# Rewriting the border between two layers: two buffers for the recurrence's heads, another order, and products moved from VectorE to GpSimd

## The reference, cut to what matters

```python
x = _layernorm(x + _L0_attn_ref(x, ...))     # causal attention, 16 heads of 8
x = _layernorm(x + _L0_ffn_ref(x, ...))      # soft mixture of 8 experts with 64 slots each
x = _layernorm(x + _L1_attn_ref(x, ...))     # delta rule: a recurrence over the 512 tokens, then an MLP
x = _layernorm(x + _L1_ffn_ref(x, ...))      # gated MLP with ternary weights
```

```python
logits = jnp.einsum('bsd,etd->bset', xn, se)
dispatch = jax.nn.softmax(logits, axis=1)
slots = jnp.einsum('bsd,bset->betd', xn, dispatch)
h = jax.nn.gelu(slots @ w1, approximate=False)
processed = h @ w2
combine = jax.nn.softmax(logits.reshape(b, s, e * t), axis=-1)
out = jnp.einsum('bnd,bsn->bsd', processed.reshape(b, e * t, d), combine)
```

```python
Sk = jnp.einsum('bhkv,bhk->bhv', Sm, ki)
upd = ki[..., :, None] * (vi - Sk)[..., None, :]
Sm = Sm + bi[..., None, None] * upd
oi = jnp.einsum('bhkv,bhk->bhv', Sm, qi)
```

## Time and profile before

| | us |
|---|---|
| median of 3 runs | 1311.79 |
| lowest, highest | 1306.53, 1312.87 |
| the profiled execution | 1302.49 |
| its span, first to last instruction | 1300.8 |

### The profile page before, as it was taken

One profiled execution on the slowest core, in us unless ns is written; L12 is line 12 of the kernel. 1 busy time (PEld: TensorE's weight loads), 2 busy tenths in 40 slices (PEclk: granted clock), 3 DMA queues, 4 the chain that ended last, 5 costly groups with the idle time before them and its releaser, 6 DMA issues.

```text
span 1300.8 us, 19019 instructions
## 1 busy us (share of the span) xinstructions
PE 1117.7 (86%) x6008; PEld 591.0 (45%) x6008; DVE 930.4 (72%) x2129; ACT 620.1 (48%) x1226; POOL 478.3 (37%) x602
## 2 busy tenths in 40 slices
PE   5989989999999999999884821297999999999996
PEld 2434444564445644455351511143545555555453
DVE  4647647477687878878575667998798898898131
ACT  1161736637456374563652300333565565555642
POOL 3040312304154341443303343444647537556310
PEclk8989999999999999999897975698999999999999
DMA  4230210322213323133022257022021120210000
GB/s 116 74 114 10 66 50 10 115 68 83 66 34 114 102 78 99 38 113 81 15 57 73 59 134 198 29 52 59 9 60 45 24 68 16 51 28 9 22 9 8
DMA packets 85043, 79.83 MB, mean 61 GB/s; under 512 B 42096, under 2 KB 62704, under 8 KB 82928
## 3 DMA queue, kind: packets, MB, share of 16 engines
q1 hardware_dynamic: 84976, 79.01, 22.0%
HBM read 43.17 MB, written 35.00 MB: 60 GB/s over the span
## 4 chain that ended last, share of the span: by engine, by line
PE 63%; DVE 17%; issue 7%; ACT 6%; POOL 4%; DMA 3%; ACTq 0%; DVEq 0%; SPq 0%; POOLq 0%
PE ps L1358 15%; PE ps L1339 7%; PE ps L1040 5%; PE ps L1001 5%; PE ps L966 5%; PE ps L1004 3%; PE ps L1011 3%; PE ps L1027 3%; PE ps L1349 3%; DVE arena L1886 2%; ACT arena L1480 2%; PE ps L1089 2%; PE ps L1069 2%; PE ps L1117 2%; PE ps L1099 2%
## 5 line engine op out<-in xcount | busy, mean ns | idle before, releaser
L1886 DVE TENSOR_REDUCE arena<-ps 128x4 f32<-128x512 f32 (+2 forms) x192 | 198.1, 1043 | 49.6 <-PE ps L1004 48.2
L1358 PE MATMUL ps<-arena,late 128*128 128x512 f32 x512 | 227.3, 596 | 0.3 <-ACT arena L1621 0.3
L1453 ACT ACTIVATE arena<-ps 128x512 f32<-128x512 f32 (+2 forms) x200 | 110.1, 568 | 239.3 <-PE ps L966 104.6
L1480 ACT ACTIVATE arena<-ps 128x1024 f32<-128x1024 f32 (+3 forms) x256 | 169.1, 712 | 32.2 <-PE ps L1027 30.9
L784 POOL TENSOR_SCALAR_AFFINE_SELECT arena<-arena 128x512 f32<-128x512 f32 x128 | 87.1, 683 | 237.4 <-ACT arena L1480 236.8
L1358 PEld LDWEIGHTS ps<-arena,late 128*128 128x128 f32 x512 | 96.2, 191 | 114.6 <-issue 112.2
L1621 ACT ACTIVATE arena<-ps,f_s 128x512 f32<-128x512 f32 x128 | 83.2, 687 | 109.3 <-PE ps L1358 98.6
L883 POOL TENSOR_TENSOR arena<-arena 128x256 f32<-128x256 f32 x128 | 93.2, 728 | 66.1 <-ACT e_w L1680 43.3
L1339 PE MATMUL ps<-arena,late 128*128 128x512 f32 x256 | 115.4, 603 | 2.1 <-ACT arena L1621 2.1
L1011 PE MATMUL ps<-mask_qk,ident_b 128*128 128x512 bf16 x340 | 91.7, 396 | 25.3 <-DVE arena L2179 25.3
L966 PE MATMUL ps<-ident,arena 128*128 128x128 f32 (+1 forms) x624 | 95.6, 286 | 18.7 <-ACT arena L1453 12.0
(11 more groups left out here) (186 smaller groups left out, 1882.9 us busy)
## 6 DMA issues: line engine op xcount, KB each, us to landing
qr<-q_rep SPq DMA_DIRECT2D x16, 512.0 KB, 4.0
kr<-k_rep SPq DMA_DIRECT2D x16, 512.0 KB, 4.9
scan_d<-late SPq DMA_DIRECT2D x7, 1104.0 KB
arena<-scan_d SPq DMA_DIRECT2D x12, 552.0 KB, 7.2
q_rep<-hilo SPq DMA_DIRECT2D x24, 256.0 KB, 3.0
k_rep<-hilo SPq DMA_DIRECT2D x24, 256.0 KB, 3.2
proj_d<-arena SPq DMA_DIRECT2D x8, 768.0 KB, 5.1
late<-proj_d SPq DMA_DIRECT2D x8, 768.0 KB, 4.5
```

Of the source, the lines that this page charges most:

```text
L1358: last = pe.matmul(ps[:, ring2.bank(f"{n}{c}"), :], w[:, k, c * P:(c + 1) * P], src[:, k, :], start=(k == 0), stop=(k == HC - 1))
L1453: return act.activation(dst, src(ps[:, bank, :]), func, **kw)
L1480: act.activation(prob[:, gg % 2, 2 * pr:2 * pr + 2, p_off[jt]:p_off[jt] + w], ps[:, bank:bank + 2, 0:w], ACT.Exp).then_inc(p_taken, 1)
L1886: v.tensor_reduce(heads[:, 2 * pr:2 * pr + 2, gs[0]:gs[-1] + 1], ps[:, at:at + 2, 0:len(gs) * w].rearrange("p q (n w) -> p q n w", w=w), X ...
```

## The change

It has four parts.

- **Two heads' buffers.** `heads_last` now serves batches 5 and 7, `heads` the others. Those two have their own `p_mix_late` in the memory of `qr` and their own `p_beta_late`, and their own semaphores (`last_loaded`, `last_stored`). Batch 7's scaling waits for batch 5's store. `raw_h2`, which shares memory with `heads_last`, is loaded after batch 7's store.
- **The slot logits first.** For batch 7 TensorE makes M0 to M3 before L0 to L3, in an order written out with its own table of banks (`border`), interleaved with the expert output and the combination of batch 6. VectorE adds batch 7's `mo` directly from PSUM (`add_last`). The hidden layer of batch 7 lies in the memory of `hilo`.
- **Older heads in the last slot.** In slot 7 VectorE folds batch 3 between the tops and sums its scores at once, makes batch 4's norms before `attend(0)` and folds batch 4 beside the last `attend`s. GpSimd squares batch 4 after its second causal selection and scales it among the last ones. The ternary weights' first three loads are issued before batch 6's store. The store of x2 has its own semaphore and comes after the heads' load.
- **First products on GpSimd.** In every batch the folding's three products `pairs` are made by GpSimd in `scale_heads`, behind the first half of `wu`; `DVE_WY` goes from 12 to 9.

```diff
+        cm = Carve(0, qr.rearrange("p g s -> p (g s)").bitcast(F32))
+        p_mix_late = cm.take(3 * HD, TS)
+        h_T_late = hilo.rearrange("p j h s -> p (j h) s").bitcast(F32)
...
+        border = {(TL, use): bank for use, bank in (
+            ("M0", 0), ("M1", 1), ("M2", 2), ("M3", 3), ("dT0", 6), ("dT1", 7), ("dT2", 0), ("dT3", 1), ("L0", 2), ("sn", 5),
+            ("L1", 3), ("L2", 6), ("slots", 7), ("L3", 0), ("h0", 1), ("h1", 2), ("h2", 3), ("h3", 5), ("cT0", 4), ("cT1", 6),
+            ("cT2", 7), ("cT3", 0), ("pr", 6), ("mo", 7))}
...
+        def beside_last(b):
+            return isinstance(b, int) and b in (B - 3, B - 1)
...
-            return heads_last if isinstance(b, int) and b == B - 2 else heads
+            return heads_last if beside_last(b) else heads
...
-            return b - 1 if isinstance(b, int) and b == B - 1 else b
+            return b - 1 if isinstance(b, int) and b >= B - 2 else b
...
             def load_heads(b):
-                sp.wait_ge(proj_stored, CREDIT + (b + 1) * 48)
-                sp.wait_ge(l_kb, CREDIT + b * 5)
-                sp.dma_start(p_mix.rearrange("p (j d) k -> p j (d k)", j=3),
+                mix, beta = mix_of(b)
+                loaded = last_loaded if beside_last(b) else pre_loaded
+                sp.wait_ge(proj_stored, CREDIT + (b + 1) * 32)
+                if mix is p_mix or b == B - 1:
+                    sp.wait_ge(l_kb, CREDIT + held(b) * 5)
+                else:
+                    sp.wait_ge(p_ready, CREDIT + B * len(p_units))
+                sp.dma_start(mix.rearrange("p (j d) k -> p j (d k)", j=3),
...
             store_heads(B - 5)
             store(B - 3)
+            store_x2(B - 3)
             load_heads(B - 3)
             store_heads(B - 4)
+            load(raw_f1, A["L1_ffn_w1_w"].rearrange("(c p) d -> p c d", p=P), raw_loaded)
+            load(raw_f2, A["L1_ffn_w2_w"].rearrange("(c p) d -> p c d", p=P), raw_loaded)
+            load(raw_w3, A["L1_ffn_w3_w"], raw_loaded)
             store(B - 2)
             load_heads(B - 2)
-            store_heads(B - 3)
+            store_x2(B - 2)
             store(B - 1)
             load_heads(B - 1)
+            store_x2(B - 1)
+            store_heads(B - 3)
...
-            sp.wait_ge(pre_stored, CREDIT + (B - 1) * 16)
+            sp.wait_ge(last_stored, 32)
             for t in range(2):
                 sp.wait_ge(sc_loaded[t], CREDIT + 48)
             load(raw_h2, A["L1_ffn_h2_w"].rearrange("(c p) d -> p c d", p=P), last_raw_loaded)
...
             def scale_heads(b):
...
                 if p is heads:
                     g.wait_ge(pre_stored, CREDIT + held(b) * 16)
+                elif b == B - 1:
+                    g.wait_ge(last_stored, 16)
+                yield g.tensor_tensor(p.kc, by_time(mix, 1), along(r_k), ALU.mult).then_inc(l_kb, 1)
+                yield g.tensor_tensor(p.wu[:, :, 0:HD], by_time(mix, 1), along(p.rb), ALU.mult).then_inc(l_kb, 1)
+                g.wait_ge(l_kb, CREDIT + b * 5 + 2)
+                g.wait_ge(wy_done, CREDIT + (held(b) if p is heads or b == B - 1 else 0) * DVE_WY)
+                for r in range(1, CH):
+                    at = r * (r - 1) // 2
+                    last = g.tensor_tensor(p.pairs[:, :, at:at + r, :], kc[:, :, 0:r, :],
+                                           wc[:, :, r, 0:HD].unsqueeze(2).broadcast_to([P, NC, r, HD]), ALU.mult)
+                yield last.then_inc(pairs_made, 1)
...
+            def last_slot():
...
+                        if (gg, jt) == (0, 1):
+                            squares_heads(B - 4, None)
+                        if (gg, jt) == (3, 0):
+                            scaled = scale_heads(B - 4)
...
+            def border_heads():
+                squares_heads(B - 3, None)
+                for _ in scale_heads(B - 3):
+                    pass
+                score_products(B - 3)
+                squares_heads(B - 2, None)
+                for _ in scale_heads(B - 2):
+                    pass
+                squares_heads(B - 1, None)
+                score_products(B - 2)
+                for _ in scale_heads(B - 1):
+                    pass
+                score_products(B - 1)
...
             def fold_heads(b, o):
-                v.wait_ge(l_kb, CREDIT + (b + 1) * 5)
-                for r in range(1, CH):
-                    at = r * (r - 1) // 2
-                    o.mark(v.tensor_tensor(p.pairs[:, :, at:at + r, :], kc[:, :, 0:r, :],
-                                           wc[:, :, r, 0:HD].unsqueeze(2).broadcast_to([P, NC, r, HD]), ALU.mult))
+                v.wait_ge(pairs_made, CREDIT + b + 1)
                 yield o.mark(v.tensor_reduce(p.gram, p.pairs, X, ALU.add))
+                v.wait_ge(l_kb, CREDIT + b * 5 + 3)
...
+            def border_tokens(fold):
+                b, last = B - 2, B - 1
+                advance(*fold, DVE_WY + 1)
+                sum_scores(B - 4)
+                for t in range(4):
+                    top(last, "M", t)
...
+                add_combined(b)
+                o = start_finish(b)
...
+                make_rms(b, o)
+                norms_heads(B - 3)
+                make_x2(b, o)
+                apply_x1(last)
...
+                fold = fold_of(B - 3)
+                advance(*fold, 4)
+                add_last()
+                o = start_finish(last)
+                make_rms(last, o)
+                norms_heads(B - 2)
+                advance(*fold, DVE_WY + 1)
+                sum_scores(B - 3)
+                make_x2(last, o)
+                fold = fold_of(B - 2)
+                advance(*fold, 6)
+                norms_heads(last)
+                advance(*fold, DVE_WY + 1)
+                sum_scores(b)
+                advance(*fold_of(last), DVE_WY + 1)
+                sum_scores(last)
```

423 lines of the change are left out of this document (328 added, 95 removed).

## The result

The changed kernel takes 1275.4 us (median of four runs, 1274.0 to 1279.7), the kernel before 1312.2: a ratio of 0.973, 95% interval 0.970 to 0.977. Forecast were 1275 and 1264 to 1290. The profiled execution of the changed kernel is one of 1274.0 us, with a span of 1272.3 and a granted clock of 0.944 (before: 1302.5, 1300.8, 0.945).

The account below looks back on a forecast made before the run. The border was taken as bound by one heads buffer passed through four batches and by VectorE's program order. 2.4 + 3 + 32.5 - 1.5 = 36.4 us less gave 1266.1 profiled, scaled to 1275 us; range 1264 to 1290.

Parts of the forecast that it names:

- Slots 4 to 6: Start of these slots: three VectorE products move to GpSimd, ending TensorE's 0.86 us waits; 2.4 us less, ends 0 and 2.6.
- The rival of engines that hold each other up: VectorE and GpSimd multiplying delay each other throughout, so moved products free little: 31.6 us gained, 1280 us; chance 14%.
- Slot 7: Last slot: TensorE's 2.15 us wait goes and shorter gaps may keep 2.4 GHz; 0 to 4 us less, 3 taken.
- The border: From slot 7's residual to the first scan step: two buffers and TensorE's continuous order save 32.5 us.
- Step 1: Border, residual to `mo`: TensorE's work sums to 39.6 us, plus 2.1 for three uncovered ScalarE evacuations; `mo` at 718.9.
- the prediction's signs of being wrong: Last heads' load over 66 us after the residual, repeated ScalarE table loads in steps 1 or 3, scan's first wait over 7.
- Step 2: Border, last tokens after `mo`: `add_last` reads PSUM directly in 1.3 us, finish without x2 takes 4.66; ends at 724.9.
- Step 3: Border, x2 transposes to the last Tanh: 5.77 us, ending at 730.7.
- Step 5: Border, squares and norms to 750.3; the last batch's scaling waits for batch 5's store, taken to land at 750.5.
- Steps 7 and 8: Border, GpSimd's scalings, score products and VectorE's last sum to 764.7, plus 2 us of mutual delay (ends 0 and 3.4): 766.7.
- Step 9: Border's end, copy to the scan tile and first scan step: 4.2 us plus 0.8 for transfers in flight; 771.7.
- `raw_h2`: Scan's eighth chunk: the history load now waits for the last batch's store; 1.5 us lost, bounds 0 and 6.5.

Follow-up runs that it names:

- before, again: The kernel before, unaltered, run once more: 1307.3 us in one execution, where its first profile took 1302.5.

## Why the prediction was right, step by step

**Slots 4 to 6: right.** Forecast 2.4 us less; undisturbed intervals of 81.03, 81.02 and 80.64 stand against 81.82, 81.86 and 81.46, 2.5 in all. The rival of engines that hold each other up would have given 0 here. Its mechanism is real wherever both multiply at the same time (below), but its price isn't: the products on GpSimd freed VectorE all the same.

**Slot 7: the size was wrong**, 1.0 in place of 3, and even this isn't clear of chance: the same stretch takes 63.6 and 61.6 us in the two profiles of before, 62.6 and 62.2 in those of the changed kernel. VectorE's 2.15 us wait went, as forecast. The first two logit records behind it came 2.2 us earlier, counted from the slot's first top, but at the slot's end 1.0 was left. Before, then the changed kernel:

```profile
618.67 0.45 PE L1027 MATMUL ps<-qr,kr 32*128 32x384 f32 x2 [1.20 <-ACT arena L1480]
```

```profile
622.75 0.44 PE L1127 MATMUL ps<-qr,kr 32*128 32x384 f32 x2 [1.20 <-ACT arena L1704]
...
625.57 2.07 PE L1169 MATMUL ps<-slot_T,arena 128*128 128x512 f32 x2
```

The waits for ScalarE just ahead are the same in both (1.20 and 0.47 us), and the clock of the stretch is 0.62 in place of 0.57, with 2.07 us for two logit records as before. One gap less didn't keep the clock; the 0 to 4.8 us for it should have been taken at the low end. A second miss stands beside it: the prediction gave slot 7 about 1 us for the products on GpSimd, and the run that put them back lost 5.5 there. The store of batch 3 was issued at 641.67, near the 640 of the forecast, and cost nothing.

**The border: right in the sum, 94.6 us against 94.5, with errors that cancel.**

| step | forecast | measured |
|---|---|---|
| 1 TensorE's order to `mo` | 41.7 | 38.7 |
| 2 `add_last`, finish | 6.0 | 7.6 |
| 3 x2 to the last Tanh | 5.8 | 7.2 |
| 4 to the squares | 11.3 | 10.2 |
| 5 to the last batch's scaling | 8.5 | 9.6 |
| 6 two scalings, products | 4.9 | 5.0 |
| 7, 8 to the last score sum | 11.3 | 11.9 |
| 9 copy, first scan step | 5.0 | 4.4 |

Step 1 added durations of groups, and these overlap by 0.1 to 0.2 us at each change:

```profile
680.43 0.60 PE L1459 MATMUL ps<-ident,arena 128*128 128x128 f32 x4
680.87 1.06 PE L1207 MATMUL ps<-e_w,arena 128*128 128x128 f32 x8
681.76 1.94 PE L1425 MATMUL ps<-arena,slot_T 128*128 128x512 f32 x4
```

The first two last 0.60 and 1.06, 1.66 together, and from the first's start to the third's it is 1.33. Over the 20 groups of step 1 the overlaps make about 2.5 us; another 1.2 is work counted too long, the transposes above all (eight take 1.04 where twice 0.65 was counted; the 14 groups named there are ten in the terms of its sum). The waits for ScalarE were 2.6 us (0.88, 0.95, 0.78) where 2.1 were taken. One of the prediction's signs of being wrong did show, two table loads of ScalarE within step 1 (at 700.64 and 708.00, 1.28 us each), and the step was short all the same; the other two signs didn't.

Step 2 left out that batch 6's squares land beside it: as the 128x4 instruction of the earlier trace rows did, another of 128x4 stood for 1.82 us, now in the last tokens' chain. It starts 0.18 us into the squares and ends with them (721.93 + 1.82, 721.75 + 1.98). The Trainium skill, page "SBUF — State Buffer", section "Who interferes with whom", says that a VectorE `tensor_scalar` in a two-port mode and a GpSimd instruction hold each other off for the whole of the one that came first; this trace and the run without that overlap (0.17 us) agree with it, though they don't show the instruction's mode. Step 3 left out that TensorE waits 2.51 us for that chain and then has a lower clock; the projections take 5.19 us where they take 3.80 with 35 idle matmuls ahead.

Step 5 was right in rule and time: the scaling waits for batch 5's store, which was issued 61.3 us after the residual (forecast 61.3) and landed 11.9 later. What held the issue is not in the prediction: SP had issued the last heads' loads by 739.98 and then waited for the store of x2, which waits for VectorE (741.18). It is longer in the table only because the squares came a microsecond early.

Steps 7 and 8 were near in time and wrong in the path. The forecast let GpSimd's queue end last (7.8 us of scalings and score products, then the sum of 1.5) and took 2 us for mutual delay, so 11.3. GpSimd's queue took 8.1 and ended at 766.65, 2.3 us before the sum began. What ended last were VectorE's own fold steps:

```profile
759.98 1.40 DVE L2265 TENSOR_TENSOR arena<-arena 128x256 f32<-128x256 f32 x1 [0.35 <-POOL arena L875]
761.41 1.45 DVE L2266 TENSOR_TENSOR arena<-arena 128x256 f32<-128x256 f32 x1
...
762.65 4.00 POOL L888 TENSOR_TENSOR arena<-arena 128x128 f32<-128x128 f32 x4
```

They took 10.3 us in place of 6.3: 3.7 of delay in the two-input steps and 0.35 of waiting. Against the forecast's 9.3 without any delay that is 2.6 more, where 2 were taken. The run with most of the last score products left out gives back 1.8 of this; the rest stands beside the three scalings. Step 9 has 0.2 us over the 4.2 of before, and 0.6 in the repeat, both with `raw_h1` 16 us ahead of the copy, and 1.7 to 2.0 with it 14 to 15 ahead, where 0.8 was taken.

So the rules of the border came out (its waits, their order up to the scaling), and the match to 0.1 us is luck: terms of 3.0 and 0.6 us too much and of 1.6, 1.4 and 0.6 too little lie beneath it.

**`raw_h2`: nothing in this profile, up to 1.2 us in others.** TensorE waited 2.08 us for it, but the history was kept at 789.8, before the eighth chunk's last step ended. In the repeat of the same kernel VectorE does wait there:

```profile
789.18 0.49 DVE L2511 TENSOR_REDUCE arena<-arena 128x64 f32<-128x320 f32 x1 [0.73 <-ACT e_w L1933]
```

and in the nine other versions of the changed kernel that step comes 0.2 to 1.2 us late. So the wait is there, as forecast, at the edge, and 1.5 us were more than any run showed. The 0.8 us of the table came later, between 74 and 194 us after the scan's start; before, again, has 0.4 of them too.

**From profile to median.** The prediction scaled by 0.7%, because the runs of before were that much above their profile, without knowing why. That profile is the only one of the 14 without a disturbed slot, the changed kernel's has three: 5.7 us. With these taken out the profiles lie 34 us apart, near the medians' 36.8; the last 2 to 3 us stay open. Scaling the sum to the median of before was right; that its profiled execution was an undisturbed one was there to be seen only beside another. Against the 34 the sum of 36.4 was 2 too much, nearly all of it slot 7's. That the forecast and the median then agree to 0.4 us is closer than any of this can be known: the ratio's interval is 10 us wide.

## What to carry over

Where buffers chain stores, an earlier start of the last batch is worth next to nothing until the chain is undone: with one buffer's waits put back, 31 of 37 us were gone although TensorE's and VectorE's new orders stayed. Whether the chain's undoing alone would have given them is not shown. Once a chain has several paths of almost the same length (here the store, the norms, the loads and the copy, within 2 us), an edit to one of them gives nothing: earlier store, full clock, early load and reordered products, four edits together, moved the first scan step by half a microsecond, less than two executions of one kernel differ by. And when two engines that hold each other up are given work side by side, check which of them ends last with the delay counted in, not before it. Before comparing two profiles, compare equal stretches of them (here first top to first top), since a single execution carries several microseconds of disturbed clock at places that are its own.

## What the runs showed of the hardware

- TensorE's granted clock fell for a few microseconds in slots of either kernel that have the same instructions and the same waits at full clock in the next execution; a disturbed slot is 1.5 to 2.7 us longer. In 14 executions the stretches of slots 1 to 6 began at two places of the slot, some 22 and some 44 us after its first top.
- A VectorE instruction of 0.17 us took 1.82 beside a GpSimd product of 1.98, and two-input steps of 0.42 took up to 2.02; GpSimd's scaling took 2.02 in place of 1.34 when VectorE came first. Reductions with one input (0.95 and 1.49 us) were the same beside GpSimd and alone.
- A 1104 KB store takes 10 us alone and 11.4 to 12.8 with other traffic; two copies of 138 KB take 3.7 to 4.3 us with a 1024 KB load issued 16 us or more ahead of them, and 5.2 to 5.7 with it 14 to 15 us ahead.
